# A four-layer attention and feed-forward program on one core: scores kept in PSUM, the ternary quantizer rewritten, and three routings issued batch by batch inside the norms

## The reference, cut to what matters

```python
# layer 0, attention: scores normed again over the keys, then softmax, added to x
kv = k_v @ W_k.T + b_k
out = einsum('bij,bjd->bid', layernorm(x), kv)
sim = einsum('bid,bjd->bij', out, kv) * 512 ** -0.5
sim = (sim - mean(sim)) * rsqrt(var(sim) + 1e-6) * ln_gamma + ln_beta
x = x + softmax(sim)
# layer 0, feed-forward: ternary weights, groups of 64, in bf16
scale = clip(mean(abs(w_g)), 1e-8, None)
w_hat = clip(round(w_g / scale), -1, 1) * scale
w_q = w + (w_hat - w)
# layers 1, 2, 3, feed-forward: a router ahead of the experts
logits = layernorm(x) @ router            # 4, 8 (and a shared gate) and 8 columns
weights = softmax over the top 2, 2 and 4 of them
```

## Time and profile before

| | |
|---|---|
| median of 3 runs | 3703.59 us (3701.0 to 3709.85) |
| the profiled execution | 3709.56 us |
| its span, first to last instruction | 3707.7 us |
| PE busy | 3084.9 us (83%) |
| DVE busy | 2243.4 us (61%) |
| ACT busy | 1801.0 us (49%) |
| POOL busy | 559.7 us (15%) |
| mean granted TensorE clock | 0.908 |

### The profile page before, as it was taken

How to read it: one execution, slowest core, us unless ns; L and a number is a source line. 1 busy time by engine, 2 the same in 40 slices (tenths; PEclk the granted TensorE clock), 3 DMA queues, 4 the chain that set the end, 5 groups by cost and what they waited for, 6 DMA issues and landing times. The chain is left out here.

```text
span 3707.7 us, 55886 instructions
## 1 busy us (share of the span) xinstructions
PE 3084.9 (83%) x15750; PEld 2116.6 (57%) x15750; DVE 2243.4 (61%) x3802; ACT 1801.0 (49%) x3122; POOL 559.7 (15%) x1150
## 2 busy tenths in 40 slices
PE   3329999879872799928998699899898899979998
PEld 2117777645461688823333388788786333338886
DVE  6974445456443333358998444566556899936655
ACT  5643333535430455525777533566533577753443
POOL 2430000024422000040111040122111011100000
PEclk7659999879985899967999799999999799979999
DMA  4424444866361433343321262576643432102333
GB/s 139 143 96 136 136 137 136 306 166 149 90 233 40 127 107 108 104 149 95 80 62 36 77 209 93 176 244 235 214 139 95 127 79 62 42 21 91 94 98 113
DMA packets 241080, 461.87 MB, mean 125 GB/s; under 512 B 57444, under 2 KB 73956, under 8 KB 240402
## 3 DMA queue, kind: packets, MB, share of 16 engines
q1 hardware_dynamic: 207602, 343.64, 30.5%
q0 software_dynamic: 22480, 96.23, 7.7%
q10 hardware_dynamic: 10864, 20.45, 1.5%
HBM read 343.78 MB, written 113.77 MB: 123 GB/s over the span
## 5 line engine op out<-in xcount | busy, mean ns | idle before, releaser
L1702 DVE TENSOR_REDUCE at_maxima<-psum 128x1 f32<-128x512 f32 (+1 forms) x768 | 620.4, 859 | 36.0 <-PE psum L1610 30.2
L1683 ACT ACTIVATE at_probs<-psum 128x512 f32<-128x512 f32 x1024 | 528.6, 604 | 208.2 <-PE psum L1626 208.2
L1626 PE MATMUL psum<-at_qT,at_kT 50*128 50x512 f32 x1024 | 375.6, 456 | 71.0 <-ACT at_probs L1683 54.3
L601 PE MATMUL psum<-f_xT_hi,ffn_w_hi 128*128 x1024 | 406.5, 397 | 10.4 <-DVE f_xT_lo L313 2.8
L601 PE MATMUL psum<-f_xT_lo,ffn_w_hi 128*128 x1024 | 406.0, 397 | 0.0
L1610 PE MATMUL psum<-at_kT,at_qT 48*128 48x512 f32 x1024 | 387.0, 482 | 12.1 <-DVE at_maxima L1702 9.7
L1626 PEld LDWEIGHTS psum<-at_qT,at_kT 50*128 50x128 f32 x1024 | 171.0, 190 | 364.3 <-ACT at_probs L1683 243.8
L1639 PE MATMUL psum<-at_probs,at_vals 128*32 128x512 f32 x2048 | 281.2, 622 | 0.0
L393 PE MATMUL psum<-ident,n_normed 128*128 128x128 f32 x512 | 102.6, 369 | 202.1 <-ACT n_normed L356 159.5
L618 PE MATMUL psum<-ffn_w_hi,ffn_hid_hi 128*128 128x512 f32 x768 | 269.2, 391 | 1.3 <-ACT ffn_hid_hi L667 1.3
L490 ACT ACTIVATE ffn_w_hi<-ffn_w_raw 128x512 fp32r<-128x512 f32 x262 | 161.7, 633 | 156.2 <-PE psum L623 101.1
(11 more groups left out here) (381 smaller groups left out, 6701.5 us busy)
## 6 DMA issues: line engine op xcount, KB each, us to landing
ffn_w_raw<-in_stream SPq DMA_DIRECT2D x262, 256.0 KB, 2.7
ffn_w_hi<-quantized SPq DMA_DIRECT2D x66, 512.0 KB, 3.6
ffn_w_hi<-quantized SPq DMA_DIRECT2D x65, 256.0 KB, 3.2
at_qT<-q_hi SPq DMA_DIRECT2D x256, 64.0 KB, 2.3
ffn2a_w_raw<-in_shared2a SPq DMA_DIRECT2D x26, 512.0 KB
qz_raw<-in_stream SPq DMA_DIRECT2D x17, 768.0 KB, 4.2
quantized<-qz_quant POOLq DMA_DIRECT2D x16, 768.0 KB, 3.5
gathered<-zeros SPq DMA_DIRECT2D x1, 12288.0 KB
```

Of the source, the lines that this page charges most:

```text
L601: mm = pe.matmul(hid_ps[h][s][0:n, :], wt[s][:, w], xt[:, c, bass.ds(b * S, S)], start=(c == 0 and i == 0), stop=(c == DC - 1 and i == len ...
L1626: pe.matmul(scoreT[turn_of(n)][:, :], kT[r][half(h % 2, USED + 2), t * P:(t + 1) * P], qT[r][half(h % 2, USED + 2), h // 2, :], start=True ...
L1683: act.activation(probs[n % RING][:, :], scoreT[turn_of(n)][:, :], ACT.Exp, scale=factor).then_inc(exped, 1)
L1702: dve.tensor_reduce(maxima[g % 2][:, h:h + banks, t], scores, AX.X, ALU.max).then_inc(maxed, 1)
```

## The change

In the attention of layer 0 the scaled scores, the logits and the exponentials are written back to the bank that holds the scores, and the next batch's scores wait for x instead of the scaled scores. The quantizer loses the limit on ACT; on DVE two operations on one tensor (half and least) and four on two tensors take the place of four. The group sums wait for the magnitude alone.

```diff
-        act.wait_ge(self.split, 6 + 3 * c + 1)
-        act.activation(self.limit[s][:, :], self.mag[s][:, :], ACT.Copy, scale=1.0 / self.OVER_HALF).then_inc(self.split, 1)
...
-        pe.wait_ge(self.split, 6 + 3 * c + 3)
+        pe.wait_ge(self.split, 4 + 2 * c + 1)
...
-        mag, scale, step = self.mag[s][:, :], self.scale[s][:, :], self.step
+        mag, scale, step, over, what = self.mag[s][:, :], self.scale[s][:, :], self.step, self.over[:, :], self.what[:, :]
...
-        dve.scalar_tensor_tensor(out=self.over[:, :], in0=scale, scalar=self.LEAST, in1=self.limit[s][:, :],
-                                 op0=ALU.max, op1=ALU.is_lt).then_inc(step, 1)
-        dve.wait_ge(step, 3 * c + 1)
-        dve.scalar_tensor_tensor(out=self.what[:, :], in0=scale, scalar=self.LEAST, in1=self.over[:, :],
-                                 op0=ALU.max, op1=ALU.mult).then_inc(step, 1)
-        dve.wait_ge(step, 3 * c + 2)
-        dve.tensor_tensor(self.what[:, :], self.what[:, :], mag, ALU.subtract).then_inc(step, 1)
-        dve.wait_ge(step, 3 * c + 3)
+        dve.tensor_scalar(self.half[:, :], scale, self.LEAST, 0.5, ALU.max, ALU.mult).then_inc(step, 1)
+        dve.tensor_scalar(self.least[:, :], scale, self.LEAST, None, ALU.max).then_inc(step, 1)
+        dve.wait_ge(step, 5 * c + 1)
+        dve.tensor_tensor(over, self.half[:, :], mag, ALU.is_lt).then_inc(step, 1)
+        dve.wait_ge(step, 5 * c + 2)
+        dve.tensor_tensor(what, self.least[:, :], mag, ALU.subtract).then_inc(step, 1)
+        dve.wait_ge(step, 5 * c + 4)
+        dve.tensor_tensor(what, what, mag, ALU.add).then_inc(step, 1)
+        dve.wait_ge(step, 5 * c + 5)
...
-        dve.tensor_tensor(self.result[s][:, :], mag, self.what[:, :], ALU.add).then_inc(self.worked, 1)
+        dve.tensor_tensor(self.result[s][:, :], what, over, ALU.mult).then_inc(self.worked, 1)
...
-                pe.wait_ge(scaled_made, TB * b + t + 1)
+                pe.wait_ge(x_made, TB * b + t + 1)
...
-                act.wait_ge(x_made, TB * b + t + 1)
-                act.activation(probs[t][:, :], logits[:, t, :], ACT.Exp, bias=minus_max[:, t:t + 1],
+                act.activation(sim[t][:, :], sim[t][:, :], ACT.Exp, bias=minus_max[:, t:t + 1],
...
-                dve.scalar_tensor_tensor(out=scaled[:, t, :], in0=sim[t][:, :], scalar=moments[:, t, 0:1], in1=gamma[:, :],
+                dve.scalar_tensor_tensor(out=sim[t][:, :], in0=sim[t][:, :], scalar=moments[:, t, 0:1], in1=gamma[:, :],
...
-                dve.scalar_tensor_tensor(out=logits[:, t, :], in0=scaled[:, t, :], scalar=rstd[:, t:t + 1], in1=beta[:, :],
+                dve.scalar_tensor_tensor(out=sim[t][:, :], in0=sim[t][:, :], scalar=rstd[:, t:t + 1], in1=beta[:, :],
...
-                dve.tensor_reduce(minus_max[:, t:t + 1], logits[:, t, :], AX.X, ALU.max, negate=True).then_inc(max_made, 1)
+                dve.tensor_reduce(minus_max[:, t:t + 1], sim[t][:, :], AX.X, ALU.max, negate=True).then_inc(max_made, 1)
...
-                dve.scalar_tensor_tensor(out=xt, in0=probs[t][:, :], scalar=inv[:, t:t + 1], in1=xt,
+                dve.scalar_tensor_tensor(out=xt, in0=sim[t][:, :], scalar=inv[:, t:t + 1], in1=xt,
```

`stage_route` becomes `weave_route`, which gives a class `Woven` to the norm and a function `weigh` for the ranking, in banks 4 to 6. In layers 2 and 3 the callers issue the norm, then the first weight splits (`start`), then `weigh`. The orders it writes:

```diff
+        def pe(pe, turn, x_made, x_before):
...
+            turn(0)
+            turn(1)
+            pe.wait_ge(w_lo_made, 1)
+            columns_of(0)
+            turn(2)
+            turn_columns(0)
+            columns_of(1)
+            turn(3)
+            for b in range(1, B):
+                turn_columns(b)
+                if b + 1 < B:
+                    columns_of(b + 1)
+            pe.wait_ge(taken, B)
...
+            apply(0)
+            act.wait_ge(landed, DMA)
+            act.activation(w_hi[:, :, :], raw[:, :, :], ACT.Copy).then_inc(w_hi_made, 1)
+            apply(1)
+            move(0)
+            apply(2)
+            move(1)
+            act.wait_ge(zeroed, 1)
+            copy_columns(0)
+            apply(3)
+            move(2)
+            copy_columns(1)
+            move(3)
+            copy_columns(2)
+            copy_columns(3)
...
+            measure(0)
+            aggregate(0)
+            measure(1)
+            make_shift(0)
+            aggregate(1)
+            dve.wait_ge(w_hi_made, 1)
+            dve.tensor_tensor(w_lo[:, :, :], raw[:, :, :], w_hi[:, :, :].bitcast(F32), ALU.subtract).then_inc(w_lo_made, 1)
+            measure(2)
+            make_shift(1)
+            aggregate(2)
+            split(0)
+            measure(3)
+            make_shift(2)
+            aggregate(3)
+            split(1)
+            make_shift(3)
+            take(0)
+            split(2)
+            take(1)
+            split(3)
+            take(2)
+            take(3)
```

More of the change, by code:

```diff
@@ L131 @@
 class Quantizer:
-    OVER_HALF = 0.5 + 2.0 ** -9
     LEAST = 1.0011717677116394e-08
@@ L146, in pair @@
             return [k.sb(ctx, f"qz_{name}{s}", [P, width], dt) for s in range(2)]
-        self.raw, self.mag, self.sign, self.limit = pair("raw", F32), pair("mag", BF16), pair("sign", BF16), pair("limit", F32)
+        self.raw, self.mag, self.sign = pair("raw", F32), pair("mag", BF16), pair("sign", BF16)
         self.scale, self.result, self.quant = pair("scale", BF16), pair("result", BF16), pair("quant", BF16)
-        self.over, self.what = k.sb(ctx, "qz_over", [P, width], BF16), k.sb(ctx, "qz_what", [P, width], BF16)
+        self.over, self.what, self.half, self.least = (k.sb(ctx, f"qz_{n}", [P, width], BF16) for n in ("over", "what", "half", "least"))
         self.groups = k.sb(ctx, "qz_groups", [P, P], BF16)
@@ new lines, in weave_route @@
+    ctx, block = room.memory, room.block
+    raw, w_hi, w_lo = k.sb(ctx, f"{nm}_raw", [P, DC, R]), k.sb(ctx, f"{nm}_w_hi", [P, DC, R], F32R), k.sb(ctx, f"{nm}_w_lo", [P, DC, R], F32R)
+    columns = k.sb(ctx, f"{nm}_columns", [P, S])
+    logits = k.sb(ctx, f"{nm}_logits", [P, NT, R])
+    beats = k.sb(ctx, f"{nm}_beats", [P, E, NT, E])
+    rank = choice if choice is not None else k.sb(ctx, f"{nm}_rank", [P, NT, E])
+    shifted, exps, chosen, kept = (k.sb(ctx, f"{nm}_{n}", [P, NT, E]) for n in ("shifted", "exps", "chosen", "kept"))
@@ new lines, in weave_route @@
+    top1, total, inv = (k.sb(ctx, f"{nm}_{n}", [P, NT]) for n in ("top1", "total", "inv"))
+    columns_ps, turned_ps = [room.banks[4 + s][0:R, :] for s in range(2)], room.tiles(6)
+    zeroed, landed, w_hi_made, w_lo_made, product, columns_made, turned, taken, compared, step, exped = k.sems(
+        ctx, nm, "zeroed landed w_hi_made w_lo_made product columns_made turned taken compared step exped")
+    if bias is not None:
+        bias_row = k.sb(ctx, f"{nm}_bias", [P, E])
+        bias_landed, = k.sems(ctx, nm, "bias_landed")
@@ new lines, in _, with over_experts, columns_of @@
+    @block.gpsimd
+    def _(pool):
+        pool.memset(columns[:, :], 0.0).then_inc(zeroed, 1)
+    def over_experts(t, n=E):
+        return t.rearrange("p (t o) -> p t o", o=1).to_broadcast([P, NT, n])
+    @block.sync
+    def _(sp):
+        sp.dma_start(raw[:, :, :], weights).then_inc(landed, DMA)
+        if bias is not None:
+            sp.dma_start(bias_row[:, :], bias.rearrange("(o e) -> o e", o=1).to_broadcast([P, E])).then_inc(bias_landed, DMA)
+    class Woven:
+        def pe(pe, turn, x_made, x_before):
+            def columns_of(b):
+                pe.wait_ge(x_made, x_before + TB * (b + 1))
+                if b > 1:
+                    pe.wait_ge(columns_made, b - 1)
@@ L1958, in _, with act, copy_columns @@
                 mm.then_inc(turned, 1)
-            pe.wait_ge(taken, B + 1)
+            turn(0)
[11 more added lines that the diff above has]
+            pe.wait_ge(taken, B)
+        def act(act, apply, move):
+            def copy_columns(b):
+                act.wait_ge(product, b + 1)
+                if b > 0:
+                    act.wait_ge(turned, b)
+                act.activation(columns[0:R, :], columns_ps[b % 2], ACT.Copy).then_inc(columns_made, 1)
+            apply(0)
[13 more added lines that the diff above has]
+            copy_columns(3)
@@ new lines, in dve, with take @@
+        def dve(dve, measure, aggregate, make_shift, split):
+            def take(b):
+                dve.wait_ge(turned, b + 1)
+                dve.tensor_copy(logits[:, b * TB:(b + 1) * TB, :], turned_ps[:, :, 0:R]).then_inc(taken, 1)
+            measure(0)
[20 more added lines that the diff above has]
+            take(3)
@@ L1961, in _, with weigh @@
+    def weigh():
         @block.scalar
         def _(act):
-            act.wait_ge(zeroed, 1)
-            act.sem_inc(turned, 1)
-            with act.Fori(0, B) as b:
-                act.wait_ge(product, b + 1)
-                act.wait_ge(turned, b + 1)
-                act.activation(columns[0:R, :], columns_ps[:, :], ACT.Copy).then_inc(columns_made, 1)
             act.wait_ge(step, 2 if bias is None else 3)
@@ L1976, in _ @@
         def _(dve):
-            with dve.Fori(0, B) as b:
```

(4 more changed lines are left out.)

89 lines of the change are left out of this document (26 added, 63 removed).

## The result

| | before | after |
|---|---|---|
| median of 4 runs | 3706.72 us | 3667.95 us (3659.74 to 3682.13) |
| ratio | | 0.9907, 95% interval [0.9884, 0.9930] |
| the profiled execution, its span | 3709.56, 3707.7 us | 3659.74, 3657.9 us |
| DVE busy | 2243.4 us | 2214.3 us |

The median lies 2 us from the forecast of 3670.0. The ratio with its interval makes 34.5 us (26 to 43) where 33.6 was forecast; the two medians differ by 38.8, and the profiled executions by 50, because the one of the kernel after is the fastest of its four.

The account below looks back on a forecast made before the run. DVE was taken to bound layer 0's attention and PE's chain of waits the routings. Attention −30.4 and routings −3.2 sum to −33.6 us, taking the median from 3703.6 to 3670.0 us, range 3657 to 3688.

Parts of the forecast that it names:

- A chunk: Layer 0 attention's quantizer on DVE: a chunk falls from 5.45 to 4.66 us, −12.7 us over 16 chunks.
- Stalls: Layer 0 attention: logits and x, with an input in PSUM, no longer wait out POOL's multiplication; −17.1 us.
- The stall that stays: Layer 0 attention: whichever DVE operation comes first behind chunk 3 still waits for POOL, 3.0 us in 3 places; +0.8 us.
- PSUM as destination: Layer 0 attention: DVE writing to PSUM costs 0; bound above +5.3 us on 32 operations.
- Scores behind x, supply: Layer 0 attention: scores waiting for x cost 0; ACT's chunk scales stay narrowly ahead, 0, bound +8 us.
- The norm 10 us longer: Norm before routing: new order of DVE waits and ACT tiles ends low part 3 at 36.3 us, not 26.4.
- The routings' sum: Three routings: −2.4 us each, less +3.0 and +1.0 given back in layers 2 and 3; −3.2 us, bounds −10 and +12.
- What the late ranking costs: Behind the routings: weight splits now delay the ranking, +3.0 us in layer 2 and +1.0 in layer 3.
- B: Rival, quantizer: tensor_scalar is no faster than tensor_tensor; +12.8 us, total 3683, chance 0.08.
- E: Rival, quantizer: rate hangs on ALU operations (max, mult, is_lt), not instruction form; +63 us, total 3733, chance 0.04.
- C: Rival, layer 0 attention: the lock with POOL stays, or scale supply replaces the stalls; +17 us, total 3687, chance 0.08.
- D: Rival, routings: PE's columns after gaps stay at 4.5 us or worse; +5 us per routing, total 3685, chance 0.10.

Follow-up runs that it names:

- quantizer_only: Kernel before with the new quantizer; scaled scores, logits and exponentials stay in SBUF. Layer 0 stretch 216.9 us against 230.9; one run.
- psum_only: Kernel before with its old quantizer, but scores kept in place in PSUM. Layer 0 stretch 212.9 us against 230.9; one run.
- moves_first: As rounding_late, with ACT taking a batch's moves ahead of the next batch's tiles; routing lengths 35.8, 35.7, 33.1 us against the changed kernel's 44.1, 44.0, 41.3.
- rounding_late: Changed kernel with DVE taking the router weights' low part behind aggregate(2), not ahead of measure(2); routing lengths 42.1, 41.9, 38.6 us against 44.1, 44.0, 41.3.
- chunks_apart: Changed kernel with other DVE work between any two quantizer chunks; layer 0 stretch 187.1 us against 199.2, batch 34.20 us against 37.06.

## Why the prediction was right

By its own steps:

1. *A chunk.* 4.66 us forecast; 125.60 − 120.95 = 4.65 in the timeline. The product of two halves, one input and bf16, held: 549 ns for 560. quantizer_only, which has the stall at L189 too, gives −14.0, where −12.7, −1.4 (the limit) and +0.8 (that stall) make −13.3.
2. *Stalls.* −17.1 forecast, −18.0 in psum_only; the 0.9 between them was not traced. Inputs in SBUF or PSUM decide, as shown. The stall that stays was right in kind: 3.44 − 0.55 = 2.89 for 3.0. It falls on L189, the second operation behind chunk 3, since the first gets in ahead of POOL. The term +0.8 was too large for it: 2.77 to 3.0 in 3 places makes 0.7, and 2.77 to 2.89 makes 0.4. The Trainium skill (SBUF — State Buffer, "Reading the diagram") counts a DVE operation in a two-port mode as a party to the lock. L189, with its one input, agrees with that, at 549 ns alone and 3439 beside POOL; its mode stands in no row.
3. *PSUM as destination.* 0 forecast; 6 ns on 32 operations are 0.2 us, and 5 ns on the logits' and maxima's reads as little. The 3.1 us that I estimated by the Trainium skill's cycle table (VectorE: DVE Perf Modes, "The TRN2 errata") are not there: a maximum takes 691 ns from PSUM for 686 from SBUF.
4. *Scores behind x, supply.* 0 and 0: no wait at the statistics. The supply has little slack left, however: the scale used at 125.60 was ready at 125.42.
5. *The norm 10 us longer.* Right in its mechanism: the last low part ends 35.5 us after the start for 26.4 before, 9.0 us longer, and moves_first and rounding_late give it back as the walk says.
6. *The routings' sum.* This was the term that was mis-sized: −3.2 forecast, about −8 measured between the two profiles (rt1 −4.5; the product in layer 2 −0.8; the low part in layer 3 −2.6). Each length fell by 3.7 to 4.5 where 2.4 was given. In layer 3 the walk gave 43.2 and 41.3 came. Of these 1.9 us, 0.6 are what I added for slow columns in batches 0 and 1. That addition was wrong in kind: batch 0's columns were slow (3.99 us), but they lie off the chain, and batch 1's took 3.05. The other 1.3 grew step by step, each step being a little shorter than I had walked it: 0.3 at measure(2), 0.4 at the first high parts, 0.8 at the end of the last low part, 1.2 at the start of batch 3's columns. On the other side, the old lengths that I started from hold a slow first batch each (4.3 to 5.3 us), and with columns of 2.94, as in quantizer_only, the old order has that much less to lose: 2.7 us in layer 3. What the late ranking costs, 3.0 and 1.0, came out at 2.9 and 1.6.

The attention's −31.7 and the routings' −8 make 40; the ratios make 34.5 and 25 (0.9907 and 0.9932), with intervals of some 9 us each way. The forecast of 33.6 lies between them. Whether the missing 6 us are scatter or something that the stages don't show can't be said from these runs. That the median came out 2 us from the forecast is therefore partly luck: both parts won more in the stages than was forecast, the whole won less than its stages, and the medians scatter by more than 2 us (the four executions after lie 22 us apart).

Of the rivals, B and E fell with 549 and 949 ns, C with L896's maximum of 754 ns, and D with the columns of 3.0 us at a granted 1.00 in batches 1 to 3 of layer 3. One reading was wrong, though nothing hung on it: of POOL's multiplications beside the three long operations only the one beside x takes 3.09 us; the one beside L194 takes 4.52.

## What to carry to other kernels

When work is woven into a stage, write down for each engine what the old order had standing ahead of the step that feeds the next batch: here the order of tiles and moves on ACT cost 5.5 to 6.3 us a norm and one early wait 2 to 2.7, so that of the 12.5 us that weaving can give in layer 3 (45.6 to 33.1) only 4.3 were left. A length that scatters between executions of the same code can hang on one slow step: take it off before two orders are compared. An operation with two SBUF inputs beside GpSimd is to be kept from starting while GpSimd runs, by an input in PSUM or by other work between (3.4 us of it were enough here). And what is moved out from under a wait has a price of its own, to be looked for in whoever comes next on its engine.

## What the runs showed of the hardware that was not expected

In layer 3 PE's granted clock did not fall in the sparser order: 1.00 for the columns of batch 1, although PE was busy for only 2.59 of the 3.79 us ahead of them, and 0.75 for batch 0, for 0.62 before. After, PE went into batch 0's columns straight from 3.65 us of turns; before, it had been idle for 2.66 us, and in quantizer_only for 1.81, with 1.00 behind it. In layer 1 batch 1's columns ran at 0.79 (3.72 us), and rt1 was 0.2 us longer for it (44.1 for 43.9). The same columns of a first batch took 2.94 us at 1.00, 4.51 at 0.62 and 5.28 at 0.50. Writing PSUM from DVE cost next to nothing (6 ns), and a bf16 operation with a single input, 549 ns long, is still held beside GpSimd, to 3439 ns. The hold goes the other way too. POOL's 10 operations of a batch took 20.86 us before, 16.30 after and 19.24 in chunks_apart, and those that are longer stand beside operations of a chunk, or of the logits, that started before them on DVE: the multiplication with 4.52 us starts 0.17 us into L191, and takes 3.32 after. No run tried this by itself, and it cost nothing, as POOL has time to spare.
